# Sequence mixer and expert layer: mixer spread over two chunk bodies, transposes taken from TensorE, norms given to GpSimd

## What is computed

```python
xn = layernorm(x)
Bu = xn @ B_w.T                      # 64 states
h = real(causal convolution of Bu with eig**t)   # per state
y = h @ C_w.T + D * xn
x = x + layernorm(y)
xe = layernorm(x)
router = softmax(xe @ w_router); gate = softmax(xe @ w_gating / 0.1)
cw = router * gate; cw = cw / (sum(cw) + 1e-9)   # 8 experts
out = sum over e of cw[:, e] * ((silu(xe @ w_gate[e]) * (xe @ w_up[e])) @ w_down[e])
x = x + layernorm(out)
```

## Time and profile before

| what | us |
|---|---|
| median of 3 runs (1153.35 to 1153.64) | 1153.64 |
| the profiled execution | 1153.37 |
| its span, first to last instruction | 1151.4 |
| TensorE busy | 1133.6 |
| VectorE busy | 915.2 |
| ScalarE busy | 703.7 |
| GpSimd busy | 622.4 |

### The profile page before, as it was taken

The page is one execution under the profiler, slowest core; times in us unless marked ns, Lnnn a source line. Parts: engine busy times, 40 slices in busy tenths (PEclk is TensorE's granted clock), DMA queues, the critical chain, the costliest instruction groups (busy, mean ns, idle before and its releaser), DMA issues.

```text
span 1151.4 us, 16819 instructions
## 1 busy us (share of the span) xinstructions
PE 1133.6 (98%) x5102; PEld 928.9 (81%) x5102; DVE 915.2 (79%) x2002; ACT 703.7 (61%) x1370; POOL 622.4 (54%) x480
## 2 busy tenths in 40 slices
PE   8999999999999999999999999999999999999997
PEld 4777888888888888888888888888888888888885
DVE  6798877878888788877878778788887888778765
ACT  6675565655656565575655666566565655756564
POOL 1386564654556455464655556455464655556453
PEclk9999999999999999999999999999999999999999
DMA  4240212102021110212102021111212102020110
GB/s 129 69 128 1 75 37 65 46 20 65 28 74 38 47 43 23 74 37 66 46 12 73 28 75 37 47 38 28 74 38 66 46 6 78 28 72 30 47 51 15
DMA packets 82713, 57.61 MB, mean 50 GB/s; under 512 B 35360, under 2 KB 64192, under 8 KB 82624
## 3 DMA queue, kind: packets, MB, share of 16 engines
q1 hardware_dynamic: 82624, 56.54, 16.8%
HBM read 48.13 MB, written 8.39 MB: 49 GB/s over the span
## 4 chain that ended last, share of the span: by engine, by line
PE 96%; DVE 1%; ACT 1%; DMA 0%; issue 0%; POOL 0%; SPq 0%; POOLq 0%; DVEq 0%; ACTq 0%
PE g L280 10%; PE u L280 10%; PE u L282 10%; PE g L282 10%; PE u L281 10%; PE g L281 10%; PE y L280 10%; PE y L282 10%; PE y L281 10%; PE n_ps L287 2%; PE m_ps L280 1%; PE m_ps L282 1%; PE m_ps L281 1%; PE m_ps L372 1%; PE m_ps L371 1%
## 5 line engine op out<-in xcount | busy, mean ns | idle before, releaser
L1125 POOL TENSOR_TENSOR hid_lo<-hid,hid_hi 128x512 fp32r<-128x512 f32 x255 | 341.3, 1338 | 416.7 <-ACT hid_hi L574 416.5
L568 ACT ACTIVATE gate<-g 128x512 f32<-128x512 f32 x512 | 305.5, 597 | 326.7 <-PE g L282 325.1
L848 DVE TENSOR_TENSOR hid<-gate,u 128x512 f32<-128x512 f32 x512 | 348.5, 683 | 165.1 <-ACT gate L568 133.9
L574 ACT ACTIVATE hid_hi<-hid 128x512 fp32r<-128x512 f32 x512 | 321.1, 627 | 38.5 <-DVE hid L848 38.0
L854 DVE TENSOR_TENSOR hid_lo<-hid,hid_hi 128x512 fp32r<-128x512 f32 x257 | 210.7, 820 | 1.8
L280 PE MATMUL g<-xe_hi,w_hi 128*128 128x512 f32 x512 | 206.4, 403 | 0.1
L280 PE MATMUL u<-xe_hi,w_hi 128*128 128x512 f32 x512 | 199.9, 390 | 1.7 <-DVE hid L848 1.7
L280 PE MATMUL y<-hid_hi,w_hi 128*128 128x512 f32 x512 | 200.1, 391 | 0.3 <-ACT hid_hi L574 0.2
L282 PE MATMUL y<-hid_hi,w_lo 128*128 128x512 f32 x512 | 199.8, 390 | 0.0
L282 PE MATMUL g<-xe_hi,w_lo 128*128 128x512 f32 x512 | 199.7, 390 | 0.0
L281 PE MATMUL g<-xe_lo,w_hi 128*128 128x512 f32 x512 | 199.6, 390 | 0.0
(11 more groups left out here) (205 smaller groups left out, 1131.7 us busy)
## 6 DMA issues: line engine op xcount, KB each, us to landing
cw_b<-cw_scratch SPq DMA_DIRECT2D x128, 256.0 KB, 3.3
x_sb<-x_in SPq DMA_DIRECT2D x16, 256.0 KB, 3.1
out_scratch<-acc_t SPq DMA_DIRECT2D x60, 64.0 KB, 2.3
ffn<-out_scratch SPq DMA_DIRECT2D x15, 256.0 KB, 2.7
x_out<-o_sb SPq DMA_DIRECT2D x15, 256.0 KB, 2.2
stage<-wgate_in SPq DMA_DIRECT2D x8, 256.0 KB, 2.9
stage<-wup_in SPq DMA_DIRECT2D x8, 256.0 KB, 3.4
stage<-wdown_in SPq DMA_DIRECT2D x8, 256.0 KB, 4.2
```

The lines of the kernel that those rows point to most:

```text
L568: nc.scalar.activation(gate[:, k % 2, :], g_ps[k % 2][:], ACT.Silu).then_inc(gate_ready, 1)
L574: nc.scalar.activation(hid_hi[:, k % RING, :], hid[:, k % RING, :], ACT.Copy).then_inc(hi_ready, 1)
L848: nc.vector.tensor_tensor(hid[:, k % RING, :], gate[:, k % 2, :], u_ps[k % 2][:], ALU.mult).then_inc(hid_ready, 1)
L1125: nc.gpsimd.tensor_tensor(hid_lo[:, k % RING, :], hid[:, k % RING, :], hid_hi[:, k % RING, :].bitcast(f32), ALU.subtract).then_inc(lo_pool, 1)
```

## The change

The mixer of a chunk is spread over two bodies. In body b the second half of chunk b+1's mixer runs (`Y_AT`: norm of y to logits and the start of the softmax) and the first half of chunk b+2's (`X_AT`: norm of x to y). Exponentials, products and weights of the softmax of chunk c are made at the start of body c (`OWN_AT`). Body 0 has the first half of chunk 1 too.

x, y and xe are no longer turned by TensorE. VectorE transposes 32x32 blocks, four DMAs store them so that they lie in the other order in DRAM, and one DMA loads them back (into `feat` or `y_tok`, in SBUF, where the readers took `n_ps` before). Only chunk 0, and y and xe of chunk 1, are still turned by TensorE. The logits are two 512-column matmuls with the router as weights; VectorE transposes the result in 32x32 blocks, so the softmax has 32 partitions with 256 elements, and the weights `cw` are transposed by VectorE also (`cw_t`, 32x512). The factor 10 of the gate is multiplied into the weights once.

Mean, variance, power and shift of all four norms of the bodies are made on GpSimd (`moments` and what calls it): seven small operations beside the power. The normalisation of x moves from VectorE to ScalarE. `x_sb` has two buffers; `z_sb` is gone, z is written to `x1`. On SyncE, the loads of experts 6 and 7 are issued later in body 0, and the load of chunk 1 earlier. The end of a chunk has `fin_turn` at block 7, `fin_stats` at 10 and `fin_norm` at 11.

```diff
-TENSOR_AT = {"turn_cw": 4, "turn_x": 5, "bu": 9, "c": 15, "turn_y": 16, "turn_xe": 26,
-             "logits": 27}
-SCALAR_AT = {"cw_t": 3, "hi_x": 8, "du": 8, "hi_w": 13, "fin_a": 19, "fin_b": 20, "z_a": 18, "z_b": 18,
-             "norm_a": 24, "norm_b": 25, "hi_xe": 26, "silus": 28}
-VECTOR_AT = {"weights": 1, "stats_x": 1, "var_x": 2, "norm_x": 3, "lo_x": 7, "enter": 8, "scan": 9,
-             "fin_turn": 6, "fin_stats": 14, "fin_var": 14, "fin_shift": 15, "leave": 12, "lo_w": 13, "y": 15, "stats_y": 16, "var_y": 16,
-             "shift": 18, "stats_x1": 22, "var_x1": 22, "shift_x1": 23, "lo_xe": 26, "softmax": 27, "exps": 30,
-             "products": 31}
-GPSIMD_AT = {"rstd_x": 2, "fin_rstd": 15, "fin_add": 21, "rstd_y": 16, "residual": 18, "rstd_x1": 22}
+X_AT = {"load_x": 0, "stats_x": 6, "norm_x": 7, "scale_x_a": 9, "scale_x_b": 10, "block_x": 12, "hi_x": 17, "du": 18,
+        "lo_x": 18, "bu": 20, "enter": 21, "scan": 22, "leave": 23, "hi_w": 25, "lo_w": 26, "c": 28, "y": 29, "block_y": 30}
+Y_AT = {"stats_y": 4, "norm_y": 5, "z_a": 7, "z_b": 8, "residual": 9, "stats_x1": 14, "norm_x1": 15, "scale_x1_a": 17,
+        "scale_x1_b": 18, "block_xe": 20, "hi_xe": 25, "lo_xe": 26, "logits": 28, "softmax": 29, "peak": 30, "silus": 31}
+FIRST_X_AT = {"scale_x_a": 0, "scale_x_b": 1, "block_x": 3, "hi_x": 7, "du": 8, "lo_x": 8, "bu": 9, "enter": 10, "scan": 10,
+              "leave": 12, "hi_w": 13, "lo_w": 13, "c": 15, "y": 15}
+FIRST_Y_AT = {"turn_y": 16, "stats_y": 16, "norm_y": 17, "z_a": 18, "z_b": 19, "residual": 19, "stats_x1": 21, "norm_x1": 22,
+              "scale_x1_a": 24, "scale_x1_b": 25, "turn_xe": 26, "hi_xe": 26, "lo_xe": 26, "logits": 28, "softmax": 29,
+              "peak": 30, "silus": 31}
+OWN_AT = {"exps": 0, "products": 1, "weights": 2}
+FIRST_OWN_AT = {"exps": 1, "products": 1, "weights": 2}
+FIN_AT = {"fin_turn": 7, "fin_stats": 10, "fin_norm": 11, "fin_a": 20, "fin_b": 21, "fin_add": 23}
+
+
+def stages(b):
+
+    if b == 0:
+        return [(1, FIRST_X_AT), (1, FIRST_Y_AT), (2, X_AT)]
+    return [(c, at) for c, at in ((b + 1, Y_AT), (b + 2, X_AT)) if c < NCHUNK]
...
+    cw_dram = nc.dram_tensor("cw_scratch", [2, E, SEQ], f32, kind="Internal").ap()
+    xn_dram = nc.dram_tensor("xn_scratch", [D, SEQ], f32, kind="Internal").ap()
+    y_dram = nc.dram_tensor("y_scratch", [SEQ, D], f32, kind="Internal").ap()
+    xe_dram = nc.dram_tensor("xe_scratch", [D, SEQ], f32, kind="Internal").ap()
...
-        x_sb, xn = sb("x_sb", [P, NT, D]), sb("xn", [P, NT, D])
+        x_sb, xn = sb("x_sb", [P, 2, NT, D]), sb("xn", [P, NT, D])
...
-        z_sb = sb("z_sb", [P, NT, D])
...
+        mix_t, feat, y_tok = sb("mix_t", [P, SEQ]), sb("feat", [P, SEQ]), sb("y_tok", [P, NT, D])
...
             def load_x(c):
-                sp.dma_start(x_sb[:], x_tok[c]).then_inc(x_loaded, 16)
+                if c >= 2:
+                    sp.wait_ge(x1_ready, c - 1)
+                sp.dma_start(x_sb[:, c % 2], x_tok[c]).then_inc(x_loaded[c % 2], 16)
...
+            def to_tokens(dram, src, done):
+                blocks = dram.rearrange("(b c) (a r) -> a c b r", c=SMALL, r=SMALL)
+                for a in range(D // SMALL):
+                    sp.dma_start(blocks[a], src[a * SMALL:(a + 1) * SMALL, :].rearrange("c (b r) -> c b r", r=SMALL)
+                                 ).then_inc(done, 16)
+
+            def to_features(dram, src, done):
+                blocks = dram.rearrange("(a r) (j b c) -> b r j a c", r=SMALL, j=NT, c=SMALL)
+                for b in range(P // SMALL):
+                    sp.dma_start(blocks[b], src[b * SMALL:(b + 1) * SMALL, :].rearrange("r (j a c) -> r j a c", j=NT, c=SMALL)
+                                 ).then_inc(done, 16)
+
...
+            def store_x_blocks(c):
+                sp.wait_ge(x_blocked, c)
+                if c > 1:
+                    sp.wait_ge(xt_loaded, 16 * (c - 1))
+                to_features(xn_dram, mix_t, x_stored)
+
+            def load_x_feat(c):
+                sp.wait_ge(x_stored, STORED * c)
+                if c > 1:
+                    sp.wait_ge(act_lo_ready, 2 * c - 3)
+                    sp.wait_ge(du_ready, c)
+                if c > 3:
+                    sp.wait_ge(xe_lo_ready, c - 1)
+                sp.dma_start(feat[:], xn_dram).then_inc(xt_loaded, 16)
...
+            def store_y_blocks(c):
+                sp.wait_ge(y_blocked, c - 1)
+                if c > 2:
+                    sp.wait_ge(y_loaded, 16 * (c - 2))
+                to_tokens(y_dram, mix_t, y_stored)
+
+            def load_y_tok(c):
+                sp.wait_ge(y_stored, STORED * (c - 1))
+                sp.wait_ge(z_ready, c)
+                sp.dma_start(y_tok[:], y_dram.rearrange("(j p) d -> p j d", p=P)).then_inc(y_loaded, 16)
...
             load_x(0)
             sp.dma_start(proj[:], proj_in).then_inc(small_loaded, 16)
             sp.dma_start(d_col[:], d_in).then_inc(small_loaded, 16)
-            for e in range(AHEAD):
+            for e in range(2):
                 load_expert(e)
-            sp.wait_ge(x1_ready, 1)
             load_x(1)
+            for e in range(2, AHEAD):
+                load_expert(e)
             load_expert(AHEAD)
             load_expert(AHEAD + 1)
 
             def body(c, par, first, last):
-                if not first and not last:
-                    sp.wait_ge(x1_ready, c + 1)
-                    load_x(c + 1)
+                if c + 2 < NCHUNK:
+                    load_x(c + 2)
                 store_cw(c, par)
                 for e in range(E):
                     spread_cw(c, par, e, first)
+                    if first and e == 0:
+                        store_x_blocks(1)
+                        load_x_feat(1)
                     if e == 3 and not first:
-                        turn_blocks(c - 1)
-                        load_blocks(c - 1)
-                    if e == E - 1 and not first:
-                        store_out(c - 1)
-                    if first and e == 0:
+                        store_fin(c - 1)
+                        load_fin(c - 1)
+                    if e == 3 and first:
                         load_expert(AHEAD + 2)
-                    if first and e == 3:
+                    if e == 5 and c + 2 < NCHUNK:
+                        store_x_blocks(c + 2)
+                        load_x_feat(c + 2)
+                    if e == 5 and first:
                         load_expert(AHEAD + 3)
+                    if e == 7 and not first and not last:
+                        store_xe_blocks(c + 1)
+                        load_xe_feat(c + 1)
+                if not first:
+                    store_out(c - 1)
+                if c + 2 < NCHUNK:
+                    store_y_blocks(c + 2)
+                    load_y_tok(c + 2)
 
...
-            def mix_logits(c, par):
+            def mix_logits(c):
                 pe.wait_ge(xe_hi_ready, c + 1)
                 pe.wait_ge(xe_lo_ready, c + 1)
-                for j in range(NT):
-                    t, at = slice(j * P, (j + 1) * P), 4 * E * j
-                    nc.tensor.matmul(m_ps[:, at:at + 4 * E], xe_hi[:, par, t], router[:], start=True, stop=False)
-                    last = nc.tensor.matmul(m_ps[:, at:at + 2 * E], xe_lo[:, par, t], router[:, 0, :], start=False, stop=True)
-                last.then_inc(logits_ready, 1)
-
-            def mix_turn_cw(c):
-                pe.wait_ge(cw_ready, c + 1)
-                nc.tensor.transpose(n_ps[:, 0:P], cw_pad[:], ident[:]).then_inc(cw_turned, 1)
+                if c > 0:
+                    pe.wait_ge(raw_read, c)
+                nc.tensor.matmul(n_ps[0:4 * E, :], router[:].rearrange("p h q -> p (h q)"), xe_hi[:, c % 2, :], start=True, stop=False)
+                nc.tensor.matmul(n_ps[0:2 * E, :], router[:, 0, :], xe_lo[:, c % 2, :], start=False,
+                                 stop=True).then_inc(logits_ready, 1)
...
+            def mix_scale_x(c, tiles):
+                if tiles[0] == 0:
...
+                for j in tiles:
+                    last = nc.scalar.activation(xn[:, j, :], x_sb[:, c % 2, j, :], ACT.Identity,
+                                                bias=shift3[:, j:j + 1], scale=rstd3[:, j:j + 1])
+                if tiles[-1] == NT - 1:
+                    last.then_inc(xn_ready, 1)
+
             def mix_hi_x(c):
-                act.wait_ge(xn_turned, c + 1)
-                nc.scalar.activation(act_hi[:], n_ps[:], ACT.Copy).then_inc(act_hi_ready, 1)
+                act.wait_ge(xt_loaded, 16 * c)
+                act.wait_ge(mixed_ready, c)
+                nc.scalar.activation(act_hi[:], feat[:], ACT.Copy).then_inc(act_hi_ready, 1)
...
+            def block_x(c):
+                dve.wait_ge(xn_ready, c + 1)
+                if c > 1:
+                    dve.wait_ge(x_stored, STORED * (c - 1))
+                if c > 2:
+                    dve.wait_ge(y_stored, STORED * (c - 2))
```

(75 more changed lines are left out.)

436 lines of the change are left out of this document (231 added, 205 removed).

## The result

| | before | after |
|---|---|---|
| median of 14 runs each, us | 1153.34 (1152.85 to 1154.26) | 1156.16 (1155.49 to 1157.83) |
| profiled execution, us | 1153.4 | 1157.8 |
| its span, us | 1151.4 | 1156.0 |

The ratio is 1.0026, interval 1.0018 to 1.0034: slower by 0.26%, or 2.8 us. Forecast were 1127 us and 0.90 for faster. The time lies outside the range of 1121 to 1141. The profiled execution is the slowest of the 14, 1.7 us above their median.

What follows compares the result with a forecast made beforehand. TensorE, busy 98% of the span, was taken to bound the kernel: 1153.4 us less 29.5 saved (14 bodies at 2.0, 1.4 in body 0, 0.1 in the last) plus 3 in body 0 gave 1127 us, range 1121 to 1141.

Steps and rivals of the forecast that it cites:

- What TensorE saves: Steady bodies 1 to 14: removing turns and narrow logits saves 1.87 to 2.14 us a body, taken as 2.0.
- The durations' 3.6 us: Rival reckoning of TensorE's transposes by duration: turns and `cw` return 3.6 us a body, giving 1099 us; chance 0.02.
- Does anything else become late?: Step checking VectorE, ScalarE, GpSimd, transfers and body 0; costed steady bodies at nothing beyond the 2.0 us saved.
- about 1 us late: VectorE's bursts from block 28 to block 2 of the next body leave it about 1 us late, within 2.2.
- 1.1 us late at worst: GpSimd in blocks 4 to 8: 10.5 us of work leave it 1.1 us late, 1.1 short of a stall.
- The 2.2 us: Spare time before `down` needs a block's result: 6.12 us until due, less 3.9 us of work between.
- priced with six others at 0.2 us more: VectorE's softmax with 256 elements a row: some 0.41 us instead of 0.221, 0.2 more on each of seven operations.
- The transfers: Stores and loads of x, xe and y take 6.9 us and fit; VectorE waits some 1.4 us at fin_stats, covered.
- Body 0: First body: x of chunk 1's chain and GpSimd's norms cost +3 us, ends -1 and +9; its savings are 1.4.
- Many small exposed waits: Rival: VectorE and GpSimd hold each other up, 0.3 to 1.4 us a body, 1131 to 1147 us; chance 0.20.
- The rival that ends slower: GpSimd's norms bound the body if small operations exceed about 0.42 us; at 0.5, some 1170 us; chance 0.06.
- the saving not had: Rival: body 0 and every body's transfers take back all of the saving, 1150 to 1156 us; chance 0.04.

Runs made afterwards that it cites:

- the run above: Kernel after the change, with the softmax's exponentials and second half of the gates in PSUM, so its products have one SBUF operand: 1144.1 us (0.9918).
- the softmax later: Kernel after the change, with exponentials, products and weights of the softmax one block later (blocks 1, 2, 3) in bodies 1 to 15: 1161.4 us (1.0069).
- Without the reciprocal: Kernel after the change, with the softmax reciprocal taken of one element per row group instead of all; leaves out part of the computation: 1144.3 us.
- the products first: Kernel after the change, exponentials multiplied before one reciprocal of 128 elements, factor of the 1e-9 term left out: 1157.6 us (1.0034).
- both cures: Kernel after the change, with softmax exponentials in PSUM, the norms moved later and x of chunk 1 turned by TensorE: 1134.3 us (0.9830).
- both bursts out: Kernel after the change, with the reciprocal of one element a row group and norm moments without four of six small operations: 1124.0 us.

## Why the prediction was wrong

*What TensorE saves* was right, and the way it was read (starts, not durations): 2.14 us a body with the waits away, against 1.87 to 2.14. The durations' 3.6 us are refuted.

*"Does anything else become late?"* is the step that failed, with "So I cost the steady bodies at nothing": two waits cost 1.95 us a body. VectorE was to be "about 1 us late"; `hid` of block 2 was 3.3 us late (394.2 to 397.48). GpSimd was to be "1.1 us late at worst", within 2.2; its `hid_lo` of block 5 ended at 407.98, 0.8 us behind 407.18, when TensorE was free for it. The 2.2 us are also worked out for `down` alone. The wait for `hid` stands at u, a deadline for which the prediction has no term; from the same timelines it leaves 397.46 - 394.2 - 0.67 = 2.6 us (an estimate). That is more than 2.2, so what went wrong is how late the engines were. Three things made them so:

1. The reciprocal was priced with six others at 0.2 us more, on a line through two other operations: a reduction that takes 0.221 for 64 elements and a transpose that takes 0.705 for 512. For five of the seven the 0.41 us were right. The reciprocal had a row of its own before, not quoted (VectorE's groups before, 106 to 1071 us):

```profile
L787 DVE RECIPROCAL e_pos<-e_pos 128x64 f32<-128x64 f32 x13 | 7.1, 546 | 0.0
```

   It is slower by the element than the others and took 1.73 for 256, 1.2 us more by itself.
2. The stretched instructions. The earlier trace rows had shown the effect on a tiny mean; the `hid_lo` of VectorE showed it too, at 0.82 us on average before where a free one takes 0.66 to 0.68. It was taken as a rival, at 0.3 to 1.4 us a body. The change put three new places in its way: `pr`, `xe_lo` and the scan. VectorE's groups after, 106 to 1071 us:

```profile
L841 DVE TENSOR_TENSOR_SCAN sum_sb<-v_sb 128x512 f32<-128x512 f32 x13 | 28.9, 2220 | 0.0
...
L879 DVE TENSOR_TENSOR xe_lo<-feat,xe_hi 128x512 fp32r<-128x512 f32 x14 | 23.7, 1694 | 0.0
...
L916 DVE TENSOR_TENSOR pr<-lg 32x128 f32<-32x128 f32 x14 | 19.1, 1366 | 0.0
```

   Before they are 1216 ns (scan), 691 ns (`xe_lo`, then from PSUM) and, with PSUM operands in the run above, 268 ns (`pr`). That is 1.0 to 1.1 us more for each, in every body. That it comes from meeting GpSimd is shown for `pr` alone, by the runs with the PSUM operands and with the softmax later. With 16 of VectorE's `hid_lo` a body at 937 ns instead of 815 in this stretch, these and the reciprocal add 1.2 + 3.1 + 16 x 0.12 = 6.2 us a body, and the second product with `trig` gives 0.4 back (1090 to 680 ns); VectorE has 37 us more where 14 x 2.8 = 39 less were forecast, 5.4 a body apart. Only `pr` and one `hid_lo` lie in the burst that TensorE ends up waiting for; that the others cost nothing on the path is inferred from the absence of a wait behind them, and was not tried.
3. The 2.2 us of spare time were given to VectorE's burst and again to GpSimd's, as if each began on time. But GpSimd's run of blocks 3 to 7 begins at 400.87, behind a `hid` of block 3 that VectorE made late (399.49). The late softmax showed what more of that lateness does: +5 us. How much of it counts in the change as it stood is less than that suggests. Without the reciprocal, and with the PSUM operands, the wait for `hid_lo` stayed at 0.78, for TensorE no longer waited for `hid` and came to the result of block 5 about as much earlier as GpSimd did. And the gains add: 8.5 us for moving the norms and 12.0 for the PSUM operands, 22 for both with x turned as well; in periods 0.67, 0.72 and 1.44. So each wait had its own cure.

*GpSimd* was priced well by the instruction where it is undisturbed: small operations 0.20 us (0.22 taken), the norm from 407.93 to 410.68, 2.7 us (2.55). Over the whole span their means are 0.20 to 0.33. In block 5 the norm took 3.4; it overlaps VectorE's instructions there, and moving the norms by one or two blocks was worth 8.5 us. "1.1 us late at worst" (1.0 by its own 10.5 and 9.5) left that out, and the late start.

*The transfers* fit better than costed: VectorE waits for `ffn` up to 1.4 us, but in ten bodies only and 4.4 us in all, where 1.4 a body were worked out, and no TensorE wait follows from it.

*Body 0* was inside its range (net +6.0 instead of +1.6). Its waits are 2.6 us for `hid` at 42.1, 2.4 for `act_lo` at 56.4 (the store and load of x, as described) with 1.4 us of slow matmuls behind it, 0.9 for `act_lo` of chunk 2 and 3.0 in three waits for `hid_lo`; before they were 3.1 us in all.

The sum by its own terms: 14 x (2.0 - 0.19) = 25.3 us not had, 4.4 more in body 0: 1127 + 29.7 = 1156.7, measured 1157.8 in the profiled execution. The last body has the wait for `hid` once more (0.6 us idle, some 0.9 by starts). Two sums of the prediction are off by 0.1 (5.2 for 4 x 1.284, and the 1.1 above); nothing hangs on them.

*The rivals.* "Many small exposed waits" named the right mechanism and the right signature (a period above 67.6 with waits for `hid` and low parts), though the long reciprocal is not in it, and was given 4 to 20 us; the waits cost 14 x 1.95 = 27. The rival that ends slower, small operations of over 0.42 us, was wrong: they took 0.20. The case that came true, the saving not had, had 0.04, and named body 0 and the transfers as what takes it back; body 0 took 4.4 of the 29.7 us, the steady bodies the rest. That the time fell beside that case's 1150 to 1156 is luck.

*What stays open.* Why the products first gained nothing alone is read from the stretched instructions, not shown by a run that lays them apart. Turning x in body 0 was worth 3.4 and 3.2 us in the two pairs that differ in it alone; in the change itself one execution does not tell. No run gave the scan and `xe_lo` an operand in PSUM, and none moved only the norm of y, so which of the three moved norms counted is not shown.

## What to carry to other kernels

Bursts on different engines that follow one another can hand their lateness on: lay them end to end in one reckoning, and beside it every moment at which something is due, the block's result and the buffer that must be free again. Price each operation from its own row, a reciprocal above all. A VectorE instruction with two SBUF operands that can meet a GpSimd instruction is to be counted some 1 us dearer, as `pr`, `xe_lo` and the scan were here; one operand in PSUM took that away for `pr`. When a change takes work off the bound engine and idle slivers appear in every period, look for the place of the hand-overs before looking for less work: one or two blocks were worth 8.5 us here.

## What was not expected of the hardware

- VectorE's reciprocal: 546 ns for 128x64, 0.94 us for 32x128, 1.73 us for 32x256. From 128 to 256 elements a row are 0.79 us, about 6 ns each, and 128x64 lies on the same line: what counts is the elements a row, not the partitions.
- Behind some waits of TensorE in body 0 six to nine matmuls start 0.43 us apart instead of 0.227, the clock's lower level of 1.2 GHz instead of 2.4. TensorE's timeline after, and the granted clock of the stretches around it:

```profile
56.36 0.47 PE L362 MATMUL m_ps<-act_hi,proj_hi 128*128 128x512 f32 x1 [2.38 <-DVE act_lo L833]
...
58.38 0.63 PE L363 MATMUL u<-xe_lo,w_hi 128*128 128x512 f32 x1
58.81 0.63 PE L364 MATMUL u<-xe_hi,w_lo 128*128 128x512 f32 x1
```
```profile
40.00:50.00 10.00, 7.89 (x35) 1.00 0.25 55
50.00:60.00 10.00, 7.62 (x29) 0.88 0.52 148
```

  Seven matmuls at 0.2 us more are 1.4 us. The length of the wait alone does not decide: such a stretch followed waits of 1.94 (exponentials in PSUM) and 2.38 us, none followed 1.94 (both cures) and 2.10 (both bursts out), nor the 2.64 at 42.11 here.
- In the kernel before, 366 small operations more on GpSimd, 85 us of it, cost 48 us, with 56 us more of VectorE's waits for the power, though GpSimd had been busy for 54% of the span.
